# A graph layer on one core: GpSimd takes the subtractions of every second quad in the normalising stage, and one semaphore carries the row statistics

## What is computed

```python
xn = layernorm(x)                      # row by row, no scale or bias
agg = segment_mean(xn[src], dst)       # 212500 gathered rows
gnn = relu(agg @ W_l.T + b_l + xn @ W_r.T) + xn
mix = linear_attention(xn, wq, bq, wk, bk, wv, bv, wo, bo)
x1 = x + gnn + mix
y = layernorm(x1)
out = x1 + layernorm(y + two_chosen_experts(y)) * gamma + beta
```

## Time and profile before

| | us |
|---|---|
| median of 3 runs | 2851.37 (2850.13 to 2856.72) |
| span of the profiled execution, first to last instruction | 2848.1 |
| median less span | 3.3 |
| busy in the span: PE / DVE / ACT / POOL | 2062.1 / 1422.9 / 955.3 / 1601.5 |
| first stage: start of the span to the first gather | 141.4 |
| of that, DVE busy in the first 135 us | 112.8 |

### The profile page before, as it was taken

How to read it: one execution, slowest core, us unless ns; L and a number is a source line. 1 busy time by engine, 2 the same in 40 slices (tenths; PEclk the granted TensorE clock), 3 DMA queues, 4 the chain that set the end, 5 groups by cost and what they waited for, 6 DMA issues and landing times.

```text
span 2848.1 us, 35328 instructions
## 1 busy us (share of the span) xinstructions
PE 2062.1 (72%) x10858; PEld 1572.0 (55%) x10858; DVE 1422.9 (50%) x3244; ACT 955.3 (34%) x2221; POOL 1601.5 (56%) x1679
## 2 busy tenths in 40 slices
PE   1067677789899876666666666666666599999998
PEld 0056555556566554444444444444444389999997
DVE  7823333345666553343343344344344367777777
ACT  4633333323333321222221221221221255555655
POOL 1077777777777777777777777777777300000000
PEclk9999989989999897887877877887877799999999
DMA  7744444344444444444444444444444222222222
GB/s 213 235 143 132 130 134 129 103 121 142 142 137 146 137 130 123 119 127 123 120 127 123 119 127 123 119 126 123 119 127 123 76 73 79 75 66 66 66 66 69
DMA packets 205191, 340.31 MB, mean 119 GB/s; under 512 B 33118, under 2 KB 151131, under 8 KB 205115
## 3 DMA queue, kind: packets, MB, share of 16 engines
q0 software_dynamic: 80160, 219.14, 27.0%
q1 hardware_dynamic: 124538, 119.81, 13.3%
q10 hardware_dynamic: 416, 0.39, 0.1%
HBM read 288.01 MB, written 51.20 MB: 119 GB/s over the span
## 4 chain that ended last, share of the span: by engine, by line
POOL 44%; PE 29%; issue 15%; DMA 4%; DVE 4%; ACT 1%; POOLq 1%; SPq 0%; ACTq 0%; DVEq 0%
POOL ring L672 44%; PE pd L1295 10%; PE pa L1280 5%; PE pc L1280 5%; DMA ring<-xn_table,idxb 3%; PE pd L1095 2%; PE pd L1079 1%; PE pa L1248 1%; PE pd L1106 1%; PE pa L1249 1%; DVE bst L1343 1%; PE pd L1088 1%; PE pd L1109 1%; PE pd L1110 1%; DVE ring L1409 0%
## 5 line engine op out<-in xcount | busy, mean ns | idle before, releaser
L672 POOL DMA_INDIRECT ring<-xn_table,idxb x1661 | 1592.7, 959 | 637.1 <-issue 486.8
L1248 PE MATMUL pa<-ring,ohh 128*128 128x256 f16 x1661 | 488.4, 309 | 570.2 <-DMA ring<-xn_table,idxb 510.7
L1248 PEld LDWEIGHTS pa<-ring,ohh 128*128 128x128 f16 x1661 | 180.9, 109 | 699.1 <-issue 497.6
L1249 PE MATMUL pa<-ring,ohh 128*128 128x257 f16 x1661 | 493.8, 313 | 0.0
L1295 PE MATMUL pd<-parts 128*128 128x256 f32 (+1 forms) x1568 | 312.1, 282 | 1.8 <-DVE parts L1748 1.8
L1295 PEld LDWEIGHTS pd<-parts 128*128 128x128 f32 (+1 forms) x1568 | 253.1, 188 | 10.3 <-DVE parts L1748 2.4
L768 ACT ACTIVATE ring<-pa 128x257 f32<-128x257 f32 x196 | 75.5, 385 | 545.5 <-PE pa L1249 545.5
L1509 DVE TENSOR_TENSOR ohh<-pc,edges 128x512 f16<-128x512 f32 (+1 forms) x307 | 211.7, 718 | 78.5 <-PE pa L1249 72.8
L1249 PEld LDWEIGHTS pa<-ring,ohh 128*128 128x128 f16 x1661 | 181.2, 109 | 104.2 <-issue 29.6
L1095 PE MATMUL pd<-mats,work 128*128 128x256 f32 x784 | 229.4, 418 | 10.8 <-ACT work L851 9.8
L1295 PE MATMUL pd<-W_lo_t,parts 128*128 128x256 f32 x784 | 219.7, 280 | 0.0
(11 more groups left out here) (205 smaller groups left out, 3475.0 us busy)
## 6 DMA issues: line engine op xcount, KB each, us to landing
ring<-xn_table,idxb POOLq DMA_INDIRECT x1661, 2.8
yT<-in_x SPq DMA_DIRECT2D x48, 512.0 KB, 4.2
xn_table<-ring SPq DMA_DIRECT2D x24, 512.0 KB, 5.4
x_rows<-work SPq DMA_DIRECT2D x48, 256.0 KB
y_rows<-work SPq DMA_DIRECT2D x48, 256.0 KB
work<-y_rows SPq DMA_DIRECT2D x24, 512.0 KB, 4.2
work<-x_rows SPq DMA_DIRECT2D x24, 512.0 KB, 3.8
out<-work SPq DMA_DIRECT2D x24, 512.0 KB, 3.1
```

What stands on the lines that cost most here:

```text
L672: pool.indirect_dma_start(out=msgs[:, k, 0:PARTS * D], out_offset=None, in_=xn_table[:, :], in_offset=bass.IndirectOffsetOnAxis(ap=idxb[:, ...
L1248: mm(pa[:, t % 2, 0:D], oh[:, slot, :], msgs[:, k, 0:D], start=begins, stop=False, skip_group_check=True)
L1249: ins = mm(pa[:, t % 2, 0:D + 1], oh[:, slot, :], msgs[:, k, D:2 * D + 1], start=False, stop=ends, skip_group_check=True)
```

## The change

The semaphore `lo_made` becomes two, one for the even steps and one for the odd. POOL takes the subtraction of the odd steps n = 1, 3, ... 23, twelve full quads, as one `tensor_tensor` of 128x1024 each, in its instruction list between the weight loads and the wait for the flag ahead of the gathers. DVE keeps the even steps: the tail (two instructions) and n = 2, 4, ... 24. Every wait on `lo_made` is written anew for the step's own semaphore. In `row_stats` the first two semaphores go, and all its steps count on the third, 14 a call.

```diff
-        RSQRT_STEPS = 3 + 3 * NEWTON
+        STATS_STEPS = 5 + 3 * NEWTON
...
             def store_parts(n):
-                sp.wait_ge(s["lo_made"], n + 1)
+                sp.wait_ge(s[f"lo_made{n % 2}"], n // 2 + 1)
...
             for t, m in ((wq_s, wq), (wv_s, wv), (wo_s, wo), (wraw[0], W_l), (wraw[1], W_r), (Wr_s, Wr)):
                 pool.dma_start(t[:, :, :], m.rearrange("(c p) n -> p c n", p=P)).then_inc(s["w_loaded"], 16)
+            for n in range(1, NQ + 1, 2):
+                pool.wait_ge(s["hi_made"], n + 1)
+                for v, r in whole(quad_of(n)):
+                    ins = pool.tensor_tensor(xp[n % XB][0:r, v, D:2 * D], xnb[n % XB][0:r, v, 0:D],
+                                             xp[n % XB][0:r, v, 0:D], ALU.subtract)
+                ins.then_inc(s["lo_made1"], 1)
...
                 act.wait_ge(s["p1_stats"], GROUP_OF[n] + 1)
-                wait(act, s["lo_made"], n - XB + 1)
+                wait(act, s[f"lo_made{n % 2}"], (n - XB) // 2 + 1)
...
                 act.wait_ge(s["rows_unscaled"], 1)
-                act.wait_ge(s["lo_made"], NQ + 1)
+                act.wait_ge(s["lo_made0"], NQ // 2 + 1)
+                act.wait_ge(s["lo_made1"], NQ // 2)
...
-            def row_stats(tiles, bn, m, r, done, value, rs, nm, fill=(), factor=1.0):
+            def row_stats(tiles, r, done, value, rs, nm, fill=(), factor=1.0):
...
-                ins.then_inc(s[bn], 1)
-                dve.wait_ge(s[bn], value)
+                ins.then_inc(s[r], 1)
+                dve.wait_ge(s[r], STATS_STEPS * (value - 1) + 1)
...
-                ins.then_inc(s[m], 1)
-                dve.wait_ge(s[m], value)
+                ins.then_inc(s[r], 1)
+                dve.wait_ge(s[r], STATS_STEPS * (value - 1) + 2)
...
-                chain, count = [RSQRT_STEPS * (value - 1)], [0]
+                chain, count = [STATS_STEPS * (value - 1) + 2], [0]
...
                 for n in TABLE_GROUPS[g]:
+                    if n % 2:
+                        continue
                     dve.wait_ge(s["hi_made"], n + 1)
                     for v, r in whole(quad_of(n)):
                         ins = V.tensor_tensor(xp[n % XB][0:r, v, D:2 * D], xnb[n % XB][0:r, v, 0:D], xp[n % XB][0:r, v, 0:D],
                                               ALU.subtract)
-                    ins.then_inc(s["lo_made"], 1)
+                    ins.then_inc(s["lo_made0"], 1)
```

More of the change, by code:

```diff
@@ L253, in build_layer @@
             flag_sum flag_added flag_set w_loaded biases_loaded wlr_turned wlr_taken bias1_set
-            x_loaded0 x_loaded1 x_loaded2 x_loaded3 p1_bn p1_mv p1_rstd p1_stats rows_unscaled hi_made lo_made xn_ready xn_stored0 xn_stored1 xn_stored2 xn_stored3 xt_turned xt_made
+            x_loaded0 x_loaded1 x_loaded2 x_loaded3 p1_rstd p1_stats rows_unscaled hi_made lo_made0 lo_made1 xn_ready xn_stored0 xn_stored1 xn_stored2 xn_stored3 xt_turned xt_made
             k_made kb_made ek_made phi_made kx_done kx_taken kxT_made kxT_taken kv_made kv_taken m_made m_taken
@@ L258, in build_layer @@
             xr_loaded0 xr_loaded1 xn2_ready xt2_turned xt2_ready q_made eq_made phq_made nrm_made nrm_eps nrm_rec qhat_made
-            cnt_max cnt_rec based o_made rl_made x1_made d_bn d_mv d_rstd d_stats
+            cnt_max cnt_rec based o_made rl_made x1_made d_rstd d_stats
             y_made yt_turned yt_ready x1_stored y_stored
@@ L263, in build_layer @@
             l2_done b2_made yin_loaded0 yin_loaded1 yb_made xb_made
-            h_made h_act o5_made z_made f_bn f_mv f_rstd f_stats zn_made f_scaled fin_made out_stored0 out_stored1
+            h_made h_act o5_made z_made f_rstd f_stats zn_made f_scaled fin_made out_stored0 out_stored1
             g_iota g_zeroed g_src_set g_loaded g_row_made g_split g_to_made g_taken g_added g_back_loaded g_mean_stored
@@ L1400, in group_stats @@
                 at_q = quads[0] * QT
-                row_stats(rows, "p1_bn", "p1_mv", "p1_rstd", "p1_stats", g + 1,
+                row_stats(rows, "p1_rstd", "p1_stats", g + 1,
                           rstd_a[:, at_q:at_q + len(rows)], nmr_a[:, at_q:at_q + len(rows)], (), XS)
@@ L1547, in middle_stats @@
                 row_stats([(x1[0:n, t * D:(t + 1) * D], n) for t, n in enumerate(rows)],
-                          "d_bn", "d_mv", "d_rstd", "d_stats", d + 1, rstd2[:, 0:2], nmr2[:, 0:2])
+                          "d_rstd", "d_stats", d + 1, rstd2[:, 0:2], nmr2[:, 0:2])
             def query_features(b):
@@ L1781, in stats_z @@
                 wait(dve, s["zn_made"], q)
-                row_stats([(z[u][0:n, t, :], n) for t, n in tiles], "f_bn", "f_mv", "f_rstd", "f_stats", q + 1,
+                row_stats([(z[u][0:n, t, :], n) for t, n in tiles], "f_rstd", "f_stats", q + 1,
                           rstd2[:, 0:len(tiles)], nmr2[:, 0:len(tiles)], fill)
```

## The result

Before: 2852.03 us (median of 8 runs). Changed: 2859.12 us (median of 8 runs, 2856.39 to 2862.07). The ratio is 1.0027, 95% interval 1.0018 to 1.0037, so the change makes the kernel slower by some 7 us, 0.27%, where 9.4 were forecast. The profiled execution has a span of 2855.4 us, 7.3 over before's.

The account below looks back on a forecast made before the run. First stage bound by DVE, carried to the end one for one: period terms sum to +9.4 us, span 2848.1 + 9.4 = 2857.5, with 3.3 between span and median 2860.8 us. The range was 2840 to 2868.

Parts of the forecast that it names:

- What bounds the kernel: First stage: DVE sets its pace, period 8.36 us, and its gains or losses carry to the end one for one.
- What is removed: First stage on DVE: twelve subtractions worth 1.13 us each, two giving nothing, so ten count, 11.3 us.
- POOL's start at 6.4: First-stage period: POOL subtracts once ACT's fp16 copy ends, 6.4 to 8.74 us; waits on it cost nothing.
- That DVE's two-input instructions are held for the whole of POOL's: First stage's small instructions: they wait out POOL's 2.34 us, net +1.21 us a period; forecast's chance 0.47.
- Which periods are held: First stage: nine held, six at +1.2 us, (12,13) at +0.7, the next two at +1.1 each.
- The size: First-stage period: 1.13 us lost and 2.34 us of POOL's subtraction gained, net +1.21, period 9.5 instead of 8.36.
- the prediction's other estimate of 2.25: POOL's subtraction: 2.25 us for 1024 columns from a skill page's 4497 ns for 2048; sum some 0.9 us less.
- The sum: Whole first stage: period terms add to +9.4 us; each 0.1 us of POOL's duration moves it some 1.0.
- The last group: Period of (24): -1.13 us for n = 21, +0.2 as the last subtraction waits for POOL's end, together -0.9.
- The cast behind the list's wait: Period (6,7): POOL's n = 5 falls into the list's wait; the cast behind may be held, +0.2 us.
- Only the scalar steps are held: Rival, first stage: two-input instructions go on beside POOL, only casts and tensor_scalar wait; -3.4 us, 2848.0; chance 0.20.
- Nothing is held: Rival, first stage: no hold, loads bind at 15.85 us for two periods; -9.8 us, 2841.6; chance 0.18.

Follow-up runs that it names:

- the doubled kernel: Changed kernel with POOL doing each of its twelve subtractions once more, ahead and into scratch: first gather 166.90 us; 3274 us on a slower chip (before 3249.5).
- the two kernels with a fill and a copy: DVE does all subtractions; at those moments POOL zero-fills scratch, or copies xnb there, against the changed kernel: first gather 145.28 and 147.54 us (142.3 without POOL's work).
- the version beside the statistics: Changed kernel, POOL's subtraction also waiting for DVE's even-step one, so starting with bn_stats: ratios to before 0.9992 and 0.9979, first gather 134.7 and 134.4 us.

## Why the prediction was right, and where it was off

- *What bounds the kernel* held: the first stage is DVE's, and on the chip of the result what it loses arrives at the end: 6.5 us at the first gather, 7.3 in the span.
- *What is removed* held: a period's statistics start 1.13 us after the first subtraction instead of 2.3. The period of n = 3 got no shorter (15.6 us against 15.4), and n = 23 gave nothing either, as the last subtraction waited for ACT in both kernels, so ten of the twelve counted.
- *POOL's start at 6.4* held (6.41), and its waits cost nothing: no store and no scaling waited for it. For the last odd step that was close: POOL ended at 139.13, 0.05 us ahead of that step's store.
- *That DVE's two-input instructions are held for the whole of POOL's* was taken without a row, by the likeness to a cast and a scalar step. It is shown now: by 1.93 to 2.02 us in six periods, by the double hold of the doubled kernel, and by the two kernels with a fill and a copy, which tell that it takes a read on POOL. The rule of the Trainium skill that was weighed (SBUF — State Buffer, section "Who interferes with whom"), by which a VectorE instruction with two SBUF inputs contends with a GpSimd instruction that reads SBUF and not with one that only writes it, agrees with all of these.
- *Which periods are held* held exactly: nine, three of them by the scalar step, with 1.64 us at the group (12,13), where 1.87 was forecast with POOL at 2.34.
- *The size* was off in two terms. POOL's subtraction takes 2.06 us, not the 2.34 scaled up from 128 columns, and under the prediction's other estimate of 2.25 as well. The prediction expected fixed costs and the second input to balance; how much is either no run shows. And a held instruction's own 0.17 us is within the 2.00, so a hold costs 1.83 more than no hold, not the whole of POOL's time. By these a full period without list work, 8.3 us before but for the flag's 0.08, is 8.3 - 1.13 + 1.83 = 9.0 us, as measured (9.00), against the forecast's 9.5.
- *The sum* came nearer than its parts, by luck. By its own rule, 1.0 us for each 0.1 of POOL, it gives 9.4 - 2.8 = 6.6 us for POOL at 2.06, and the first gather was 6.5 later. But the eleven periods gave only 5.0 of that and the last subtraction's wait 0.5. The other 0.9 had no term: 0.3 lies ahead of group (2,3), where traces of one kernel differ by as much, and 0.6 behind the last subtraction.
- *The last group* was wrong in its mechanism: the last subtraction was not held by POOL, it waited for ACT (2.64 us by the row above, 0.96 in the earlier trace rows). With DVE's short last period, ACT is still at the copy of step 23 until 136.78 and scales step 24 from 136.68 instead of at once. That cost 0.5 us where 0.2 stood. From the start of the last subtraction to the first gather it then took 7.97 us, before 7.36; that was not foreseen, and its cause stays open.
- *The cast behind the list's wait*, counted with 0.2, was not held: POOL had ended 0.2 us ahead of it. That period is 0.26 us longer all the same, by a later landing of the list.
- *Rivals.* "Only the scalar steps are held" is what POOL's fill does, not its subtraction. The 692 ns of the products between the gathers, which spoke for it, fit that, if a gather's instruction on POOL reads no tensor, as the prediction took it; no run shows what it reads. "Nothing is held" falls, but its second half, the bound by loads at 15.85 us for two periods, is real, and binds once the hold is gone (16.1 measured).

## What to carry to other kernels

Before work goes from VectorE to GpSimd, look at what VectorE is doing at the very moment GpSimd will read SBUF: even the smallest two-input or scalar instruction waited here for all that was left of GpSimd's, and a chain of small dependent instructions is a bad place for that. One more wait, which moved most of GpSimd's instructions beside one-input work, turned 6.5 us lost into over 7 us gained in the first stage here, against the kernel in which VectorE does all. When a bound is lifted, work out the next one from the trace first; here it was the distance from a buffer's release to the landing of its next load.

## What the runs showed of the hardware

- A VectorE instruction with two SBUF inputs, of 8 columns, took 1.93 to 2.02 us beside a GpSimd subtraction (2.06 us) and 0.97 to 1.05 beside a GpSimd copy (1.04 us), but 0.17 beside a GpSimd fill (1.81 us). A `tensor_scalar` took up to 1.64 us beside the fill and, in the changed kernel, 1.64 to 2.03 beside the subtraction.
- `bn_stats`, one input, is not touched by any of them: 2.69 to 2.71 us for eight, with GpSimd beside it and without.
- GpSimd for 128x1024: 2.06 us for fp32 minus fp16 to fp16, 1.04 us for an fp32 copy. VectorE takes 1.22 us for that subtraction.
- The order counts both ways. In the version beside the statistics, VectorE once had a long two-input instruction under way, and GpSimd's subtraction, 0.2 us behind it, took 3.58 us: 1.5 more than its own 2.06, where 1.67 were left of VectorE's. In the changed kernel the last one began with 0.37 us left of VectorE's subtraction and took 2.28. Beside a `tensor_reduce` of 1.88 us, one input, it kept to 2.06.

```profile
76.27 1.89 DVE L1464 SCALAR_TENSOR_TENSOR yT<-edges,yT 128x1666 f32<-128x1666 f32 x1
76.49 3.58 POOL L663 TENSOR_TENSOR ring<-yT,ring 128x1024 f16<-128x1024 f32 x1 [8.27 <-DVE ring L1420]
```
